# One-hot builds of a graph edge count: even widths, scalar compares for the targets, and no ScalarE share

## The reference

```python
x, src, dst = ...            # (625, 768), 20,000 edges, sorted by dst
e = leaky_relu(alpha_src[src] + alpha_dst[dst], 0.2)
m = segment_max(e, dst);  e = exp(e - m[dst]);  s = segment_sum(e, dst)
out = segment_sum(xl[src] * (e / (s[dst] + 1e-16))[:, :, None], dst) + bias
```

## Time and profile before

| | us |
|---|---|
| median of 3 runs (lowest, highest) | 1215.29 (1214.89, 1217.29) |
| the profiled execution, whole | 1210.92 |
| its span in the trace | 1208.9 |
| the stage of the counts, 22.4 to 142 of the span | 119.6 |
| PE, DVE, ACT busy in that stage | 109.3, 86.1, 80.2 |

### The profile page before, as it was taken

One profiled execution on the slowest core, in us unless ns is written; L12 is line 12 of the kernel. 1 busy time (PEld: TensorE's weight loads), 2 busy tenths in 40 slices (PEclk: granted clock), 3 DMA queues, 4 the chain that ended last, 5 costly groups with the idle time before them and its releaser, 6 DMA issues.

```text
span 1208.9 us, 19245 instructions
## 1 busy us (share of the span) xinstructions
PE 1059.0 (88%) x6178; PEld 660.8 (55%) x6179; DVE 752.7 (62%) x1289; ACT 558.7 (46%) x740; POOL 340.1 (28%) x184
## 2 busy tenths in 40 slices
PE   5989778999889759989989308999999999999997
PEld 3555467646656546556768204555555555555554
DVE  7677678783545863449966428793114989879611
ACT  2676557303131234238843027772114778778511
POOL 3100000290003322116001327652001656566400
PEclk9999889999989979989999658999999999999999
DMA  8920200022401440020000389995002999999500
GB/s 302 370 74 1 104 1 1 1 105 77 79 1 64 79 79 1 1 101 2 2 2 1 81 210 387 373 360 215 13 26 66 356 353 398 359 385 368 209 13 29
DMA packets 98379, 170.63 MB, mean 141 GB/s; under 512 B 38612, under 2 KB 38692, under 8 KB 98331
## 3 DMA queue, kind: packets, MB, share of 16 engines
q1 hardware_dynamic: 88138, 145.33, 34.6%
q0 software_dynamic: 6016, 16.80, 4.5%
q10 hardware_dynamic: 4176, 7.87, 2.1%
HBM read 153.19 MB, written 18.79 MB: 142 GB/s over the span
## 4 chain that ended last, share of the span: by engine, by line
PE 66%; DVE 16%; issue 7%; ACT 4%; DMA 2%; DVEq 2%; POOL 1%; POOLq 0%; ACTq 0%; SPq 0%
PE psum L1333 30%; PE psum L1532 14%; PE psum L1553 13%; DVE area L1274 4%; PE psum L1370 2%; PE psum L1322 2%; PE psum L1541 2%; DMA sorted_tokens<-area,smalls 2%; DVE smalls L923 1%; PE psum L1449 1%; DVE low L935 1%; DVE area L1179 1%; PE psum L1528 1%; DVE low L1039 1%; DVE low L1040 1%
## 5 line engine op out<-in xcount | busy, mean ns | idle before, releaser
L1333 PE MATMUL psum<-area,low 128*125 128x256 f16 (+2 forms) x1080 | 251.7, 395 | 21.2 <-DVE low L1118 10.9
L1274 DVE TENSOR_TENSOR area<-low,area 128x1536 f16<-128x1536 f32 x96 | 223.1, 2366 | 19.2 <-ACT area L852 19.1
L637 POOL TENSOR_TENSOR area<-low,area 128x1536 f16<-128x1536 f32 x48 | 184.5, 3843 | 156.7 <-ACT area L852 156.5
L852 ACT ACTIVATE area<-low 128x1536 f16<-128x1536 f32 x144 | 209.8, 1482 | 36.5 <-DMA low<-in_L_ffn_W_dram 29.8
L1532 PE MATMUL psum<-area,low 128*128 128x512 f16 x972 | 221.4, 382 | 0.0
L1553 PE MATMUL psum<-area,low 128*128 128x384 f16 x1296 | 217.9, 326 | 0.6 <-issue 0.3
L1333 PEld LDWEIGHTS psum<-area,low 128*125 128x125 f16 (+1 forms) x1080 | 151.9, 152 | 116.0 <-issue 65.6
L1553 PEld LDWEIGHTS psum<-area,low 128*128 128x128 f16 x1296 | 126.4, 98 | 80.2 <-issue 1.6
L1333 PE MATMUL psum<-area 125*128 125x64 f16 (+9 forms) x1076 | 145.4, 287 | 16.3 <-DVE area L1260 8.0
L1532 PEld LDWEIGHTS psum<-area,low 128*128 128x128 f16 x972 | 95.7, 98 | 114.6 <-issue 4.3
L1333 PEld LDWEIGHTS psum<-area 125*128 125x128 f16 (+3 forms) x1076 | 94.1, 128 | 51.2 <-issue 14.1
(11 more groups left out here) (205 smaller groups left out, 1295.5 us busy)
## 6 DMA issues: line engine op xcount, KB each, us to landing
low<-in_L_ffn_W_dram SPq DMA_DIRECT2D x144, 768.0 KB, 7.1
area<-in_L_gnn_W_dram SPq DMA_DIRECT2D x2, 3072.0 KB, 11.9
area<-in_L_gnn_Wr_dram SPq DMA_DIRECT2D x2, 3072.0 KB, 16.1
sorted_tokens<-area POOLq DMA_DIRECT2D x3, 1792.0 KB, 16.5
sorted_totals<-area POOLq DMA_DIRECT2D x3, 1792.0 KB, 28.7
low<-sorted_tokens ACTq DMA_DIRECT2D x11, 384.0 KB, 3.2
low<-sorted_totals ACTq DMA_DIRECT2D x9, 384.0 KB, 3.7
area<-in_L_ffn_Wv_dram SPq DMA_DIRECT2D x6, 384.0 KB, 6.3
```

The costliest lines, as they stand in the source:

```text
L637: pool.tensor_tensor(low_, raw_view(u), high_, ALU.subtract).then_inc(pool_low_ok, 1)
L852: act.activation(unit_parts(u)[0], raw_view(u), ACT.Copy).then_inc(high_ok, 1)
L1274: dve.tensor_tensor(low_, raw_view(u), high_, ALU.subtract).then_inc(dve_low_ok, 1)
L1333: ins = pe.matmul(place(name)[0:parts, at:at + w], left(q), right(q)[:, at:at + w], start=(q == 0), stop=(q == k - 1))
```

## The change

- VectorE builds all four source one-hots of a group (j = 0 to 3). ScalarE's loop, its scratch area `distance` and its semaphores go away; what is left on ScalarE is the copy of xl1 and the mask.
- The four target one-hots are no longer one tensor_tensor but four tensor_scalar compares, written in turn with the source ones.
- Source one-hots are NP = 626 columns wide and target one-hots PP = 126, and the target's slice of `iota16` begins at an even column. For odd blocks the one-hot therefore has a column too many in front, and TensorE reads it one column further on. `iota16` is filled to 626 columns.
- TensorE waits for VectorE alone.

```diff
-            act.wait_ge(bounds_r, 1)
...
-                with act.Fori(0, groups) as i:
-                    act.wait_ge(src_act_ready[d], i + 1)
-                    act.activation(distance[:, 0:N], iota16[:, 0:N], ACT.Abs, scale=-1.0,
-                                   bias=eT[:, 0, J - 1, bass.ds(lo + i, 1)]).then_inc(distance_ok[d], 1)
-                    act.wait_ge(distance_ok[d], i + 2)
-                    act.sem_inc(act_turn, 1)
-                    act.wait_ge(oh_used[d], i + 1)
-                    act.activation(oh_src[:, bass.ds(i % AHEAD_G * (J * NP) + (J - 1) * NP, N)], distance[:, 0:N],
-                                   ACT.Relu, scale=-1.0, bias=ones[0:P, 0:1]).then_inc(src_act_ready[d], 1)
                 copy(("xl1", d), xl1[:, d, :], place(("xl1", d), HC, P))
...
-                columns = iota16[:, P * d:P * d + P]
-                columns = bass.AP(tensor=columns.tensor, offset=columns.offset, ap=[columns.ap[0], [0, J], [1, P]])
+                columns = iota16[:, P * d - P * d % 2:P * d - P * d % 2 + PP]
                 with dve.Fori(0, groups) as i:
                     dve.wait_ge(oh_used[d], i + 1)
                     dve.sem_inc(dve_turn, 1)
-                    dve.tensor_tensor(v3(oh_dst[:, bass.ds(i % AHEAD_G * (J * 128), J * 128)], J)[:, :, 0:P], columns,
-                                      eT[:, 1, :, bass.ds(lo + i, 1)].broadcast_to([P, J, P]), ALU.is_equal)
-                    for j in range(J - 1):
-                        ins = dve.tensor_scalar(oh_src[:, bass.ds(i % AHEAD_G * (J * NP) + j * NP, N)], iota16[:, 0:N],
+                    for j in range(J):
+                        dve.tensor_scalar(oh_dst[:, bass.ds(i % AHEAD_G * (J * 128) + j * 128, PP)], columns,
+                                          eT[:, 1, j, bass.ds(lo + i, 1)], None, ALU.is_equal)
+                        ins = dve.tensor_scalar(oh_src[:, bass.ds(i % AHEAD_G * (J * NP) + j * NP, NP)], iota16,
                                                 eT[:, 0, j, bass.ds(lo + i, 1)], None, ALU.is_equal)
                     ins.then_inc(oh_ready[d], 1)
...
                     pe.wait_ge(oh_ready[d], i + 1)
-                    pe.wait_ge(src_act_ready[d], i + 2)
                     for j in range(J):
-                        targets = oh_dst[:, bass.ds(i % AHEAD_G * (J * 128) + j * 128, P)]
+                        targets = oh_dst[:, bass.ds(i % AHEAD_G * (J * 128) + j * 128 + P * d % 2, P)]
```

## The result

| | before | changed |
|---|---|---|
| median of 19 runs (lowest, highest), us | 1212.67 (1207.39, 1217.29) | 1218.67 (1214.93, 1223.74) |
| ratio to the runs of before, 95% interval | | 1.0048 (1.0034 to 1.0063) |
| span of the profiled execution | 1208.9 | 1218.7 |
| first group of block 0 to last group of block 4 | 105.28 | 111.19 |

The changed kernel is slower by 0.48%, 5.8 us (4.1 to 7.6). The two profiled executions differ by 9.8 us, of which the last row has 5.9.

What follows compares the result with a forecast made beforehand. TensorE's instruction stream was taken to pace the loop. With VectorE's turn at 2.03 us, blocks 1 to 4 add 1.7, block 0 0.95 and the end 0.1: 1215.29 + 2.75 = 1218.0 us, range 1212.5 to 1222.5.

Steps and rivals of the forecast that it cites:

- What paces the loop before: In the group loop, TensorE's instruction stream sets the 1.84 us turn, with both builders ahead by about a microsecond.
- Even widths worth nothing: VectorE's source compares: 625 columns already run at fp16's doubled rate, 0.295 us start to start; a 626th brings nothing.
- The estimate of 0.09: Alternative price of a 126-column compare on VectorE, from 58 fixed cycles; it would lower the sum by 1.5 us.
- VectorE's stream becomes the pace: Four added pairs lengthen VectorE's loop turn from 1.36 to 2.03 us, over TensorE's 1.74, so TensorE waits each turn.
- The pair of address instruction and compare: Each target compare with its address instruction takes 0.167 us of VectorE's stream; the change adds four per turn.
- The sum: Added stage time: blocks 1 to 4 +1.7 us, block 0 +0.95, the stage's end +0.1, together +2.75.
- the ring's opening: VectorE may build a block's fifth group once TensorE finishes the first, at 13.85 us; VectorE gets there at 13.5.
- The end: From the last group's start to the count's copy after the reductions: 2.5 us instead of 2.39, +0.1.
- TensorE keeping the pace: TensorE's stream still sets the group loop's turn, at 1.74 us; 1212.4 us in total, chance 0.15.
- all five loops get block 0's long turn: VectorE's loops all turn at 2.27 us; 1224.4 us, or 1219.6 to 1221.2 for one or two loops; chance 0.17.
- the third rival: Block 0's early VectorE builds collide with GpSimd's issues, costing 0 to 2 us, up to 1220; chance 0.04.
- The fourth rival: VectorE's loop turn comes out near 1.92 us and the time stays at 1215.3; chance 0.12.

Runs made afterwards that it cites:

- scalar targets alone: The kernel before, ScalarE still building the last source one-hot, but with target one-hots as four scalar compares of 126 columns; ratio 1.0026.
- the narrow: The changed kernel with source compares of 126 columns instead of 626 and the ring zeroed at the start; 1274.84 us, not comparable because edges are left out.
- the padded kernel: The kernel before with 7 empty semaphore instructions added to each turn of VectorE's loop; ratio 1.0033.
- 18 instructions ahead: The changed kernel with 18 empty semaphore instructions on VectorE ahead of its first loop; ratio 1.0034 to the kernel before.
- one target instruction: The changed kernel with the four target one-hots again one tensor_tensor, VectorE still building all source one-hots; ratio to the kernel before 0.9983, timed again 0.9961.
- 30 instructions ahead: The changed kernel with 30 empty semaphore instructions on VectorE ahead of its first loop; one execution, 1219.56 us.

## Why the prediction was right, and where its size was off

**What paces the loop before: right.** The reading that TensorE's stream, not ScalarE, sets 1.84 us was borne out twice: taking all work and the wait for ScalarE away gained only 2.5 us, with groups 1.77 apart (1.74 was predicted) and "issue" in the brackets, and adding to VectorE's turn up to 1.93 cost nothing in blocks 1, 2 and 4 of the kernel with scalar targets alone.

**Even widths worth nothing: right**, 399 against 400 ns. The compare of 126 columns, priced at 0.165 from start to start, came at 0.16 to 0.17. The estimate of 0.09 from the Trainium skill ("VectorE: DVE Perf Modes", The TRN2 errata) was too low; here the measurement decides.

**VectorE's stream becomes the pace: right**, and shown by the narrow and the padded kernel. The pair of address instruction and compare was priced at 0.167, and that is what it costs. The turn came out at 2.09, not 2.03, since the first address instruction of a turn grew: in a steady turn of block 1 it takes 0.216 us at L983 and took 0.134 at L1002 (0.230 and 0.144 in the block's first turn, the longest in the rows above). This term was missing from the sum. Why the same kind of instruction takes longer there, no run tells.

**The sum: too small.** The term that was mis-sized is the length of the blocks: +0.95 + 1.7 predicted, +4.3 measured. The 0.06 us a turn, on the 16 turns after the fifth group of blocks 1 to 4, are 1.0 of the missing 1.6 (block 0's turn was priced at 2.27 and took 2.29, 0.06 in all). In block 3 the sixth group comes 1.93 after the fifth instead of 1.75, because VectorE reaches the ring's opening late, by the little that the prediction gave as slack (13.5 against 13.85); that is 0.2 more. The last 0.4 are some 0.1 in each block ahead of the steady turns: in block 1 the fifth build began 1.76 after the first group instead of 1.68 (58.63, 60.39) and took 1.99 instead of 1.92, of which TensorE gave some back by following 0.31 behind the last one-hot instead of 0.39. The end, +0.1, was right. So the stage costs 4.5 us, and 2.75 was forecast. That what follows moves with the stage was right within the noise: in the padded kernel the stage grew by 3.8 us and the time by 4.0, with 18 instructions ahead by 3.7 and 4.1.

**The number 1218.0 was in part luck.** It lies 0.7 from the measured 1218.67, but it was built on 1215.29, the median of three runs, and the median of 19 is 1212.67. The base was 2.6 too high and the added term 3.1 too small, and the two errors nearly cancel. What the prediction had right is the sign and the mechanism; of the loss it had half, 2.75 of 5.8.

**What was not in the prediction at all** is the fall of the clock after block 0, 1.4 to 1.5 us in two of four traces, 0.7 on average over so few. With it the traces explain some 5.2 of the 5.8 us; the interval begins at 4.1, so nothing more need be there, though these runs don't exclude it.

**The rivals.** TensorE keeping the pace fell: its spacing was VectorE's. That all five loops get block 0's long turn did not come true in the changed kernel, but the mechanism is real, and shifting the code by 30 instructions put block 2 into it. The early builds of block 0 did get slow, as the third rival had it: VectorE's source compares took up to 1.00 us between 27 and 33.6, 0.38 later. But they were over in time. VectorE sat idle before its fifth build, waiting for the ring, so they cost nothing:

```profile
30.45 1.00 DVE L985 TENSOR_SCALAR area<-area 125x626 f16 x1
...
34.60 0.38 DVE L985 TENSOR_SCALAR area<-area 125x626 f16 x1
35.74 0.26 DVE L983 TENSOR_SCALAR area<-area 125x126 f16 x1 [0.77 <-PE psum L1350]
```

Whether GpSimd's issues are what slowed them, no run tells. The fourth rival, a turn near 1.92 and no change, fell with the turn of 2.09. One of the prediction's readings was wrong and had no part in the sum: VectorE's digits in slices 2 to 5 of the earlier trace rows are 6, 7, 7, 6, not 6, 7, 8, 6.

## What to carry to other kernels

In a loop whose offsets depend on its counter, count the instructions of each engine's stream first: there every small operation brings an address instruction, and one wide instruction with broadcast operands can beat four narrow ones though its execution is hardly shorter (0.59 against 4 x 0.165 = 0.66 us here, but 1.52 us a turn of the stream against 2.09). An engine with the longest busy time per turn is not the pace while a ring gives it a lead; look at whose bracket says "issue". The lead must last to the loop's end, though: ScalarE's, with 2.04 us a turn against 1.84, shrank from 1.9 us at the sixth group of block 1 (60.54, 62.45) to 1.1 at the tenth (68.71, 69.83), and at 0.2 us a turn would have been gone some five turns later (an estimate). A change of a tenth of a microsecond a turn is worth nothing or all of it, depending on which stream is longer, so work out the crossing point before the edit (here 1.92 us by the prediction's sum; a turn of 1.93 cost nothing in three blocks).

## What the runs showed of the hardware that was not expected

- The same loop costs VectorE 0.2 us more a turn when it lies across certain places of the engine's instruction stream. Counted by VectorE's rows in the traces, each loop once, the loops with long turns are those that contain the 64th instruction (block 0 in all kernels but the two with the shifts) or the 192nd (block 3 with one target instruction and with scalar targets alone, block 2 with 30 instructions ahead), each with the one before it. Eighteen empty instructions ahead took block 0 from 2.29 to 2.09; thirty brought block 2 to 2.32. The extra time stands at two points of the turn: 0.11 to 0.12 us on the step to that instruction (in the changed kernel's block 0, 0.279 between two address instructions that are 0.166 apart in block 1) and 0.08 to 0.10 behind the closing branch (0.27 to 0.29 instead of 0.19). No loop here lay across the 128th instruction, and those across the 256th (block 4 of the changed kernel) had no extra time. Why it is these places, no run tells.
- A wait of TensorE for 0.9 us in each turn of 2.29 was followed by half the clock for 3.4 us in some executions, and not in others of the same kernel.
- A compare of 126 columns in fp16 takes 0.25 us by itself and 0.165 to the next start, one of 625 or 626 columns 0.38 and 0.29. By this, 500 columns more cost 0.125 us to the next start, which leaves 0.13 us of each that doesn't depend on the columns (an estimate): most of the short compare, less than half of the long one.
- An empty semaphore instruction took 0.093 us of VectorE's stream (seven of them in the padded kernel).
